# The first attention of a four-layer kernel: division moved behind the weighted values, the first block's scores a turn ahead, and the copies and the rotation dealt anew

## The chip, the cores and the metric

One core of one Trainium2 chip. The metric is the device time of one execution in microseconds (us); before the change it is 1525.61 us, the median of 3 runs (1525.4 to 1527.39). The engines go by their names in the profile: PE is TensorE (PEld its loading of weights), DVE is VectorE, ACT is ScalarE, POOL is GpSimd, SP is the engine that issues most transfers. Each engine works through its own queue in order, and queues meet only in semaphores.

## What is computed

The reference is a network of four layers over 4 sequences of 256 tokens, 512 wide. Each layer is a norm, an attention and a feed-forward part, and they differ. Only the attention of the first layer is touched:

```python
def _L0_attn_ref(x, wq, wk, wv, wo):
    # B, T, C = 4, 256, 512; n_head = 32, h = 16
    q, k, v = (proj(wq), proj(wk), proj(wv))
    q = _apply_rope(q, sin, cos)      # x * cos + rot(x) * sin
    k = _apply_rope(k, sin, cos)
    scores = jnp.einsum('bnth,bnsh->bnts', q, k) * (1.0 / math.sqrt(h))
    scores = jnp.where(causal, scores, -jnp.inf)
    attn = jax.nn.softmax(scores, axis=-1)
    out = jnp.einsum('bnts,bnsh->bnth', attn, v)
    ...
    return jnp.einsum('btc,dc->btd', out, wo)
```

## The kernel before

The program is written by hand, engine by engine, with semaphores; nothing is scheduled by a planner. A phase ends where all engines meet in `finish`. Phase 1 is the first norm, phase 2 the first attention, phase 3 the first feed-forward part.

Phase 2 goes over `NB` = 4 blocks (a block is one sequence of 256 tokens) and, in each, over `G0` = 8 groups `g` of four heads. One group of one block is a turn, `t = 8 b + g`; there are 32. PSUM has 8 banks. A turn uses them so:

- banks 0 and 1: scores of the first 128 tokens (`tb` = 0, the early half, which sees 128 keys); banks 2 and 3: those of the other 128 tokens (`tb` = 1, the late half, 256 keys)
- bank 5, left half: the projection of a unit; right half: the values, or a quarter of the product with `wo` for an earlier block (a "piece")
- banks 5, 6 and 7: the transposed probabilities; banks 6 and 7 also the transposed stacks
- bank 4: the weighted values of a pair of turns, even and odd, four heads each. The first turn of a pair clears the bank and so waits until the last pair was taken away (`ot`).

A unit is the projection of 128 tokens to q or k for half of the heads; `prepared(b, g)` says which unit is made in turn `(b, g)`, five turns ahead of its use. The last five turns of the last block make none. Values are made in turns `g` = 1, 2, 5 and 6 (`VALUES`), pieces in the turns that `quarter` names (3, 4 and 7 of the second block; 0, 3, 4 and 7 of the third; 0 and 3 to 6 of the last).

In a turn of before, PE makes the scores and then masks them with four products (L1544), transposes the probabilities of the turn before (L1526), projects a unit and makes values or a piece (L1573 to L1581), transposes the stacks of the earlier unit (L1477) and makes the weighted values (L1490). ACT copies the first block of transposed probabilities out (`A_pT`, L677), takes the exponentials with their sums (L694), copies the transposed stacks to `qT` or `kT` (L671), the values (L662), the projection with its halves swapped (`A_sw`, L646) and the stack of the rotated unit (L654). POOL multiplies `A_sw` by the sines (L477). DVE takes the row minima (`least`, L1052; the scores are negated, so the minimum is subtracted), the rests of the stack (L1018), the other two blocks of transposed probabilities (L1024), divides the probabilities by their sums (L1061 to L1066), adds a piece to `X` (L1030), multiplies by the cosines (L1005, `A_T1`, which the profile calls `A_T`) and adds sines and cosines (L1011, `A_q`), and every second turn copies the weighted values to `OT0` (L1042).

Copies on ACT all go through one helper and so all have the line L598. The products of the projection have the lines L347 to L349 of `product3`. The second `OT0` and the second buffer of probabilities lie in `raw` and go by that name in the profile.

SP stages the normed tokens of the next block once the last unit that reads the old ones is projected (L369), and starts to load the weights of phase 3 when all units are projected (L404). In the last block DVE, POOL and ACT also prepare the first weights of phase 3 (`unpack`, `scale_tile`, `ffn_heads`, `weight_rests`).

Of the kernel before, what the change touches and what calls it, by code (L numbers as in the profile page):

```python
# [13 lines left out]
def build_program(nc, d, out):  # L14
# [8 lines left out]
    P = 128  # L23
    C = 512
# [24 lines left out]
    with ctx:  # L49
# [41 lines left out]
        with phase() as early:  # L91
# [3 lines left out]
            zq = sb(early, "zq", [NF, C], I32)  # L95
# [6 lines left out]
            with phase() as st:  # L102
# [20 lines left out]
                A_sum = sb(st, "A_sum", [P, 8])  # L123
                A_rec = sb(st, "A_rec", [P, 8])
# [153 lines left out]
        a = sems("a", "stage0 stage1 init proj sw t1 t2 q hi lo tp ev vps vcp sc least exp rec pn pt pe pd pv ot wo_ps x")  # L278
# [77 lines left out]
        def _(sp):  # L356
# [12 lines left out]
            def stage(b):  # L369
                for tl in range(2):  # L370
                    if not isinstance(b, int) or b >= 1:
                        sp.wait_ge(a["proj"], b * G0 + (tl - 1))
                    else:
                        ln_wait(sp, 0, "lo", tl + 1)
# [29 lines left out]
            sp.wait_ge(a["proj"], G0 * NB)  # L404
# [53 lines left out]
        def _(pool):  # L458
# [17 lines left out]

            def sines(U, tl, is_k):  # L477
                pool.wait_ge(a["sw"], U + 1)
                nc.gpsimd.tensor_tensor(A_sw[:, :, :], A_sw[:, :, :], rope0s[:, is_k, tl, :].unsqueeze(1).broadcast_to([P, H0 // 2, D0]), ALU.mult)\  # L479
                  .then_inc(a["t2"], 1)  # L480

            def attend(b):
                for g in range(G0):
                    unit = prepared(b, g)
                    if unit:
                        sines(unit[0], *unit[3:])

            for g in FIRST:
                unit = prepared(-1, g)
                sines(unit[0], *unit[3:])  # L490
            for b in range(NB):
                attend(b)

# [102 lines left out]
        def _(act):  # L596
# [49 lines left out]
            def swap_halves(unit):  # L646
                U = unit[0]
                act.wait_ge(a["proj"], U + 1)
                after(act, a["q"], U)
                ps = PS[:, 5, 0:HALF].rearrange("p (h d) -> p h d", h=H0 // 2)  # L650
                copy(A_sw[:, :, 0:D0 // 2], ps[:, :, D0 // 2:D0])
                copy(A_sw[:, :, D0 // 2:D0], ps[:, :, 0:D0 // 2], a["sw"])

            def stack_heads(unit):  # L654
                U, _, _, _, is_k = unit
                act.wait_ge(a["q"], U + 1)
                after(act, a["tp"], U)
                copy(STK[:, :, 0:D0].bitcast(F32R), A_q[:, :, :])
                at = 2 * D0 if is_k else D0
                copy(STK[:, :, at:at + D0].bitcast(F32R), A_q[:, :, :], a["hi"])  # L660

# [1363 lines left out]
```

## Time and profile before

| | |
|---|---|
| median of 3 runs | 1525.61 us (1525.4 to 1527.39) |
| the profiled execution | 1527.51 us |
| its span | 1525.5 us |
| mean granted clock of PE | 0.972 |
| PE busy | 1391.6 us (91%) |
| DVE busy | 1046.1 us (69%) |
| ACT busy | 735.5 us (48%) |
| POOL busy | 433.2 us (28%) |

The profiled execution is one run of its own; rows come from it, so sums are made against its 1527.51 us. "Busy" counts an engine's instructions, overlapping ones once. In a timeline a group of equal instructions stands in one row, with the time of its start and the time from the first one's start to the last one's end; behind it stands the idle time of the engine ahead of the row and the instruction that ended it. Products on PE overlap: one shows about 0.28 us, but the next may start 0.11 or 0.12 us after it. The chain of waits follows the work that ended last back from its end, at each step to what released it. The granted clock is 1.00 at full speed.

### The profile page before, as it was taken

Reading aid. Unit: us, or ns where it says so; the run is one execution under the profiler, and the core shown is the slowest. Engines: PE = TensorE matmul, PEld = TensorE weight load, DVE = VectorE, ACT = ScalarE, POOL = GpSimd, SP = SyncE. Lnnn points to the kernel's source line nnn. Section 1 sums busy time; section 2 is a strip of 40 time slices with the busy share of each in tenths; the row PEclk is TensorE's granted clock in tenths of the full one; section 3 lists DMA queues with packets and bytes.
Section 4 is the critical chain, followed back from the end, with each engine's and each line's share of the span. In section 5 each row is a group of like instructions: output and inputs, shape, how many; then the busy total and the mean of one; then the engine's idle time right before and its main releaser. Section 6 shows DMA issues by size and latency. Waiting matters only on the chain.

```text
span 1525.5 us, 26083 instructions
## 1 busy us (share of the span) xinstructions
PE 1391.6 (91%) x9252; PEld 1202.8 (79%) x9252; DVE 1046.1 (69%) x2049; ACT 735.5 (48%) x1996; POOL 433.2 (28%) x328
## 2 busy tenths in 40 slices
PE   3889999899999696989999999999999999948998
PEld 2777777667777584879898999899998999837887
DVE  6688778959999644456676666676666766763554
ACT  3777777622222222336556565556555665522332
POOL 5100000122222641324343442414343443224000
PEclk9999999989999897799999999999999999979999
DMA  6101020212230001111212120010212120010000
GB/s 207 29 2 29 1 71 2 84 63 102 105 117 0 21 0 35 45 35 28 70 29 69 28 69 27 21 48 28 69 28 69 28 69 28 0 63 7 15 14 28
DMA packets 39687, 67.92 MB, mean 45 GB/s; under 512 B 4940, under 2 KB 13799, under 8 KB 39618
## 3 DMA queue, kind: packets, MB, share of 16 engines
q1 hardware_dynamic: 37522, 65.69, 13.7%
q10 hardware_dynamic: 2096, 1.33, 0.3%
q8 instruction: 41, 0.67, 0.2%
q14 instruction: 28, 0.23, 0.0%
HBM read 60.68 MB, written 2.13 MB: 41 GB/s over the span
## 4 chain that ended last, share of the span: by engine, by line
PE 71%; issue 9%; DVE 8%; ACT 6%; POOL 4%; DMA 1%; SPq 0%; POOLq 0%; DVEq 0%; ACTq 0%
PE PS L347 18%; PE PS L349 17%; PE PS L348 17%; PE PS L1833 2%; PE PS L1482 2%; PE PS L1820 2%; PE PS L1819 2%; PE PS L1818 2%; POOL E_sw L546 1%; DVE ln_xn L937 1%; ACT A_p L694 1%; POOL A_sw L479 1%; PE PS L1522 1%; ACT A_pT L598 1%; PE PS L1426 1%
## 5 line engine op out<-in xcount | busy, mean ns | idle before, releaser
L347 PE MATMUL PS<-XNH,E_WL 128*128 128x256 f32 x768 | 215.8, 281 | 6.6 <-POOL E_WL L462 5.8
L349 PE MATMUL PS<-XNH,E_WH 128*128 128x256 f32 x768 | 214.8, 280 | 0.0
L348 PE MATMUL PS<-XNL,E_WH 128*128 128x256 f32 x768 | 214.3, 279 | 0.0
L546 POOL TENSOR_TENSOR E_sw<-E_sw,rope2s 128x1024 f32<-128x1024 f32 x64 | 105.0, 1641 | 267.6 <-ACT E_sw L598 267.6
L1259 DVE TENSOR_REDUCE E_nb<-PS 128x4 f32<-128x512 f32 x64 | 61.3, 958 | 163.4 <-PE PS L1820 163.4
L347 PEld LDWEIGHTS PS<-XNH,E_WL 128*128 128x128 f32 x768 | 144.5, 188 | 11.0 <-POOL E_WL L462 8.8
L348 PEld LDWEIGHTS PS<-XNL,E_WH 128*128 128x128 f32 x768 | 144.5, 188 | 1.0
L349 PEld LDWEIGHTS PS<-XNH,E_WH 128*128 128x128 f32 x768 | 144.2, 188 | 0.0
L462 POOL TENSOR_TENSOR E_WL<-raw,E_WH 128x512 fp32r<-128x512 f32 x80 | 102.7, 1313 | 131.9 <-ACT E_WH L598 131.9
L598 ACT ACTIVATE E_sw<-PS 64x256 f32<-64x256 f32 (+1 forms) x128 | 89.4, 699 | 104.6 <-PE PS L349 103.1
L808 ACT ACTIVATE E_p<-PS,E_nb 128x128 f32<-128x128 f32 (+1 forms) x256 | 104.2, 420 | 35.4 <-DVE E_nb L1259 35.4
L347 PE MATMUL PS<-E_WH,OL 128*128 128x512 f32 x256 | 103.4, 404 | 1.4 <-DVE OL L1329 1.4
L349 PE MATMUL PS<-E_WH,OH 128*128 128x512 f32 x256 | 100.6, 393 | 0.0
L348 PE MATMUL PS<-E_WL,OH 128*128 128x512 f32 x256 | 100.0, 390 | 0.0
L500 POOL TENSOR_TENSOR F_w<-F_t,scb 128x512 f32<-128x512 f32 x33 | 48.5, 1469 | 133.2 <-DVE F_t L990 133.2
L479 POOL TENSOR_TENSOR A_sw<-A_sw,rope0s 128x256 f32<-128x256 f32 x32 | 23.2, 725 | 212.5 <-ACT A_sw L598 212.5
L1269 DVE TENSOR_SCALAR E_p<-E_p,E_rec 128x128 f32<-128x128 f32 (+1 forms) x256 | 79.7, 375 | 2.3
L598 ACT ACTIVATE PH<-PS 128x512 fp32r<-128x512 f32 x64 | 52.0, 812 | 58.8 <-PE PS L1833 58.8
L1426 PE MATMUL PS<-ident,ln_xn 128*128 128x128 f32 x128 | 29.2, 373 | 52.9 <-DVE ln_xn L937 52.9
L1818 PE MATMUL PS<-QKH,QKL 128*128 128x256 f32 x256 | 74.9, 293 | 0.0
L1820 PE MATMUL PS<-QKH 128*128 128x256 f32 x256 | 72.6, 284 | 0.0
L1312 DVE TENSOR_TENSOR PL<-PS,PH 128x512 fp32r<-128x512 f32 x64 | 61.1, 956 | 16.6 <-ACT PH L598 15.3
(269 smaller groups left out, 4113.3 us busy)
## 6 DMA issues: line engine op xcount, KB each, us to landing
raw<-in_w SPq DMA_DIRECT2D x104, 256.0 KB, 2.9
words<-in_words SPq DMA_DIRECT2D x11, 768.0 KB, 4.2
wo<-in_wo SPq DMA_DIRECT2D x32, 256.0 KB, 3.9
zb<-z_scratch SPq DMA_DIRECT2D x11, 384.0 KB, 4.8
scb<-in_scales SPq DMA_DIRECT2D x11, 384.0 KB, 5.6
X<-in_x SPq DMA_DIRECT2D x8, 256.0 KB, 5.6
SGH<-XNH SPq DMA_DIRECT2D x8, 256.0 KB, 2.7
SGL<-XNL SPq DMA_DIRECT2D x8, 256.0 KB, 2.8
```

Source lines behind the costliest of these rows:

```text
L347: nc.tensor.matmul(o, sl, mh, start=first, stop=False, **shared)
L348: nc.tensor.matmul(o, sh, ml, start=False, stop=False, **shared)
L349: return nc.tensor.matmul(o, sh, mh, start=False, stop=last, **shared)
L462: nc.gpsimd.tensor_tensor(lo, raw[:, slot, :], f32(hi), ALU.subtract).then_inc(w_lo, 1)
L546: nc.gpsimd.tensor_tensor(E_sw[:, heads, :], E_sw[:, heads, :], rope2s[:, :].unsqueeze(1).broadcast_to([P, heads.stop - heads.start, SEQ]) ...
L598: ins = nc.scalar.activation(o, i, ACT.Copy)
L808: last = nc.scalar.activation(E_p[:, blocks, :].rearrange("p n t -> p (n t)"), PS[:, 3 + 2 * tb + h // 2, at:at + (tb + 1) * P], ACT.Exp, ...
L1259: V.tensor_reduce(E_nb[:, 4 * tb:4 * tb + 4], PS[:, 3 + 2 * tb:5 + 2 * tb, :].rearrange("p n (h s) -> p (n h) s", h=2)[:, :, 0:(tb + 1) * ...
L1269: last = V.tensor_scalar(E_p[:, blocks, :], E_p[:, blocks, :], E_rec[:, 4 * tb + h:4 * tb + h + 1], None, ALU.mult)
L1312: V.tensor_tensor(PL[:, n, :], PS[:, 3 + n.start:3 + n.stop, :], f32(PH[:, n, :]), ALU.subtract)\
L1818: mm(o, QKL[:, h, t], QKH[:, 4, :], start=False, stop=False, skip_group_check=True)
L1820: last = mm(o, QKH[:, h, t], QKH[:, 4, :], start=False, stop=True, skip_group_check=True)
```

## The change

- **Division.** The probabilities are no longer divided by their sums. `A_sum` and the new `A_inv` hold the sums of both turns of a pair. After the pair's second turn DVE inverts them (`invert_sums`) and spreads each over 16 columns (`A_rec`, which lies in the enlarged `zq`); PE transposes that into the right half of bank 4 (`sums`, in the even turns); DVE copies the reciprocals into `OT0` and multiplies them by the weighted values (`take_outputs`, now in the odd turns from the fourth on, ahead of `invert_sums`).
- **Scores.** PE makes the masks first and the scores on top. The early half of turn t + 1 is made in turn t, behind the stack transposes; the late half stands at the turn's start. ACT and DVE take their halves in that order.
- **Pieces and values** are made behind the stacks' transposes and the early scores, once the projection has been read. They have signals of their own (`vps`, `wo_ps`).
- **Rotation.** DVE multiplies by sines and cosines straight from PSUM (`turn_heads`); POOL adds (`rotate`) and makes the rests (`stack_rests`); DVE makes both copies of the stack in one instruction (`stack_heads`).
- **Copies.** The values of a turn are copied by DVE, those of the first five units still by ACT.
- SP waits for `vps` in place of `proj`.

The core of the diff:

```diff
 POOL
+            def rotate(unit):
+                U = unit[0]
+                pool.wait_ge(a["t1"], U + 1)
+                pool.wait_ge(a["t2"], U + 1)
+                after(pool, a["lo"], U)
+                nc.gpsimd.tensor_tensor(A_q[:, :, :], A_T1[:, :, :], A_sw[:, :, :], ALU.add).then_inc(a["q"], 1)
+
+            def stack_rests(unit):
+                U, _, _, _, is_k = unit
+                pool.wait_ge(a["hi"], U + 1)
+                at = D0 if is_k else 2 * D0
+                nc.gpsimd.tensor_tensor(STK[:, :, at:at + D0], A_q[:, :, :], STK[:, :, 0:D0], ALU.subtract).then_inc(a["lo"], 1)
 ACT
+            def exponentials(t, tb):
+                e = t % 2
+                act.wait_ge(a["least"], t * 2 + (tb + 1))
+                after(act, a["pt"], t * 2 - 2)
+                if e == 0 and tb == 0:
+                    after(act, a["inv"], t // 2)
...
             def attend(b):
                 for g in range(G0):
+                    t, earlier = b * G0 + g, prepared(b, g, 1)
+                    exponentials(t, 0)
+                    if t:
+                        take_first(t)
+                    exponentials(t, 1)
                     if earlier:
                         take_stacks(earlier)
-                    if unit and g in VALUES:
-                        act.wait_ge(a["proj"], unit[0] + 1)
-                        take_values(unit, 5, 1)
-                    if unit:
-                        swap_halves(unit)
-                        stack_heads(unit)
 DVE
+            def turn_heads(unit):
                 U, _, _, tl, is_k = unit
+                dve.wait_ge(a["proj"], U + 1)
+                after(dve, a["q"], U)
+                ps = PS[:, 5, 0:HALF].rearrange("p (h d) -> p h d", h=H0 // 2)
+                half = D0 // 2
+                for at in (0, half):
+                    ins = V.tensor_tensor(A_sw[:, :, at:at + half], ps[:, :, half - at:D0 - at],
+                                          rope0s[:, is_k, tl, at:at + half].unsqueeze(1).broadcast_to([P, H0 // 2, half]), ALU.mult)
+                ins.then_inc(a["t2"], 1)
+                V.tensor_tensor(A_T1[:, :, :], ps, rope0c[:, is_k, tl, :].unsqueeze(1).broadcast_to([P, H0 // 2, D0]), ALU.mult).then_inc(a["t1"], 1)
...
+                both = STK[:, :, 0:at + D0].rearrange("p h (n d) -> p h n d", d=D0)[:, :, 0:at // D0 + 1:at // D0, :]
+                V.tensor_copy(both.bitcast(F32R), A_q[:, :, :].unsqueeze(2).broadcast_to([P, H0 // 2, 2, D0])).then_inc(a["hi"], 1)
...
+            def take_values(unit, n):
+                _, b, half, _, tl = unit
+                dve.wait_ge(a["vps"], n)
...
             def take_outputs(t):
-                dve.wait_ge(a["pv"], t)
+
                 n = t // 2 - 1
-                V.tensor_copy(OT0s[n // KT % 2][:, n % KT, :], PS[:, 4, 0:SEQ]).then_inc(a["ot"], 1)
+                out = OT0s[n // KT % 2][:, n % KT, :]
+                dve.wait_ge(a["rt"], n + 1)
+                V.tensor_copy(out, PS[:, 4, SEQ:2 * SEQ]).then_inc(a["r"], 1)
+                dve.wait_ge(a["r"], n + 1)
+                V.tensor_tensor(out, out, PS[:, 4, 0:SEQ], ALU.mult).then_inc(a["ot"], 1)
...
+            def invert_sums(t):
+                n = t // 2 + 1
+                dve.wait_ge(a["exp"], t * 2 + 2)
+                V.reciprocal(A_inv[:, :, :, :], A_sum[:, :, :, :]).then_inc(a["inv"], 1)
+                dve.wait_ge(a["inv"], n)
+                after(dve, a["rt"], n - 1)
+                V.tensor_copy(A_rec[:, :, :, :, :], A_inv[:, :, :, :].unsqueeze(4).broadcast_to([P, 2, 4, 2, D0])).then_inc(a["rec"], 1)
 
             def attend(b):
                 for g in range(G0):
...
+                    least(t, 1)
+                    if t:
+                        take_second(t)
+                    if unit:
+                        turn_heads(unit)
+                    if t + 1 < NB * G0:
+                        least(t + 1, 0)
+                    if unit:
+                        stack_heads(unit)
+                    if unit and g in VALUES:
+                        take_values(unit, values_before(b, g) + 1)
+                    elif piece:
+                        add_quarter(*piece, quarters_before(b, g) + 1)
+                    if g % 2 == 1 and t > 1:
+                        take_outputs(t - 1)
+                    if g % 2 == 1:
+                        invert_sums(t)
 PE
+            def sums(t):
+
+                pe.wait_ge(a["rec"], t // 2)
+                for tb in range(2):
+                    last = nc.tensor.transpose(PS[:, 4, SEQ + tb * P:SEQ + (tb + 1) * P],
+                                               A_rec[:, tb, :, :, :].rearrange("p c e d -> p (c e d)"), ident[:, :])
+                last.then_inc(a["rt"], 1)
...
+                    scores(t, 1)
                     if t:
                         probabilities(t, g - 1, earlier, prepared(b, g, 2))
                         pe.wait_ge(a["pe"], t)
                     if unit:
-                        last = project(unit)
-                        if g in VALUES:
-                            last = values(unit)
-                        elif piece:
-                            last = output_quarter(*piece, False)
-                        last.then_inc(a["proj"], 1)
-                    elif piece:
-                        output_quarter(*piece, True).then_inc(a["wo_ps"], 1)
+                        project(unit).then_inc(a["proj"], 1)
                     if earlier:
                         after(pe, a["pd"], t)
                         transposes(earlier)
+                    if t + 1 < NB * G0:
+                        scores(t + 1, 0)
+                    if unit and (g in VALUES or piece):
+                        pe.wait_ge(a["t1"], unit[0] + 1)
+                        pe.wait_ge(a["t2"], unit[0] + 1)
+                    if unit and g in VALUES:
+                        values(unit).then_inc(a["vps"], 1)
+                    elif piece:
+                        output_quarter(*piece, not unit).then_inc(a["wo_ps"], 1)
                     if t:
                         weighted_values(t, (g - 1) % G0, b * KT + (g - 1) // 2)
+                        if g % 2 == 0:
+                            sums(t)
```

## Rows read from the trace of the kernel before

**Rows 1.** Busy time by stretch, the 32 turns: length, PE, PEld, DVE, ACT, POOL, clock, DMA, GB/s.

```profile
52.00:303.00 251.00, 222.54 (x2044) 181.73 (x2042) 206.16 (x522) 182.15 (x707) 23.40 (x30) 0.99 0.10 33
```

**Rows 2.** Chain of waits in one turn: start us, length us, what.

```profile
161.67 0.35 ACT A_sw L598 x2
162.09 0.73 POOL A_sw L479
162.90 0.44 DVE A_q L1016
...
164.00 0.57 ACT A_pT L598
```

**Rows 3.** Timeline of PE, one turn with values: start us, us, what [idle before].

```profile
164.61 0.39 PE L347 MATMUL PS<-WQH,SGL 128*128 128x256 f32 x1 [0.50 <-ACT A_pT L598]
...
167.59 1.03 PE L1482 MATMUL PS<-ident,STK 128*128 128x128 f32 x8
168.56 0.64 PE L1502 MATMUL PS<-A_pT,V 128*32 128x256 f32 x8
...
169.35 0.73 PE L1550 MATMUL PS<-kT,qT 64*128 64x128 f32 x8
170.00 0.61 PE L1555 MATMUL PS<-mask_ts,identb 128*128 128x256 bf16 x4
170.97 1.50 PE L1540 MATMUL PS<-ident,A_p 128*128 128x128 f32 x12 [0.36 <-DVE A_T L1008]
172.98 0.39 PE L347 MATMUL PS<-WQH,SGL 128*128 128x256 f32 x1 [0.50 <-ACT A_pT L598]
```

**Rows 4.** Timeline of PE in a turn of the last block without a unit.

```profile
278.58 1.47 PE L1540 MATMUL PS<-ident,raw 128*128 128x128 f32 x12
279.89 1.97 PE L1522 MATMUL PS<-wo,OT 128*128 128x256 f32 x8
```

**Rows 5.** Timeline of DVE: row minima, `A_pT`, division of four blocks, outputs.

```profile
163.24 1.82 DVE L1052 TENSOR_REDUCE A_nb<-PS 128x4 f32<-128x512 f32 x2
...
165.30 1.22 DVE L1028 COPY A_pT<-PS 128x1024 f32<-128x1024 f32 x1
...
166.64 0.88 DVE L1065 TENSOR_SCALAR A_p<-A_p,A_rec 128x128 f32<-128x128 f32 x4
...
171.60 0.42 DVE L1045 COPY raw<-PS 128x256 f32<-128x256 f32 x1
```

**Rows 6.** Chain of waits: a turn's exponentials, a piece, a copy of stacks.

```profile
84.66 3.17 ACT A_p L694 x16
...
141.33 1.73 PE PS L1522 x8
...
143.97 1.03 ACT kT L598
```

**Rows 7.** Timeline of PE: the scores that begin turns 1, 9 and 29.

```profile
51.55 0.72 PE L1550 MATMUL PS<-kT,qT 64*128 64x128 f32 x8 [1.11 <-ACT kT L598]
...
113.02 0.72 PE L1550 MATMUL PS<-kT,qT 64*128 64x128 f32 x8 [0.37 <-issue]
...
277.48 0.72 PE L1550 MATMUL PS<-kT,qT 64*128 64x128 f32 x8 [0.33 <-ACT kT L598]
```

**Rows 8.** Busy time by stretch, the end of the stage, columns as in rows 1.

```profile
305.00:310.00 5.00, 3.01 (x22) 2.08 (x24) 2.51 (x5) 0.60 (x1) 0.00 (x0) 0.54 0.00 0
310.00:315.00 5.00, 4.37 (x17) 1.88 (x10) 0.42 (x1) 0.00 (x0) 0.00 (x0) 0.50 0.00 0
```

**Rows 9.** Chain of waits: the last product with `wo`.

```profile
311.26 9.28 PE PS L1513 x16
```

**Rows 10.** Timeline of DVE and POOL at the start of phase 3, side by side.

```profile
322.08 0.69 DVE L990 TENSOR_TENSOR F_t<-F_q,zb 128x512 f32<-128x512 int32 x1
322.95 1.44 POOL L500 TENSOR_TENSOR F_w<-F_t,scb 128x512 f32<-128x512 f32 x1 [1.39 <-DVE F_t L990]
323.40 1.53 DVE L990 TENSOR_TENSOR F_t<-F_q,zb 128x512 f32<-128x512 int32 x1
```

More of the change, by code:

```diff
@@ L475, in _ @@
             pool.wait_ge(const_in, 16 * 9)
[L477 to L482, printed above, removed]
+            def rotate(unit):
[9 more added lines that the diff above has]
+                nc.gpsimd.tensor_tensor(STK[:, :, at:at + D0], A_q[:, :, :], STK[:, :, 0:D0], ALU.subtract).then_inc(a["lo"], 1)
+            for g in FIRST:
+                unit = prepared(-1, g)
+                rotate(unit)
+                stack_rests(unit)
+            for b in range(NB):
                 for g in range(G0):
@@ L485, in attend @@
                     if unit:
[L486 to L492, printed above, removed]
+                        rotate(unit)
+                        stack_rests(unit)
             def scale_tile(n, p):
@@ L644, in ffn_heads, with take_values @@
                     copy(FWH[p][:, c, :], F_w[:, c, :], f["hi"])
[L646 to L660, printed above, removed]
-            def take_values(unit, bank, side):
-                U, b, half, _, tl = unit
-                if b >= 1:
-                    act.wait_ge(a["pv"], b * G0 + (4 * half - 4))
-                ps = PS[:, bank, side * HALF:(side + 1) * HALF].rearrange("p (k e j d) -> p k e j d", k=2, e=2, j=4)
+            def take_values(unit):
+                _, _, half, _, tl = unit
+                ps = PS[:, 3, 0:HALF].rearrange("p (k e j d) -> p k e j d", k=2, e=2, j=4)
                 for e in range(2):
@@ L681, in take_probabilities @@
                 copy(A_pT[:, 0:4, :], PS[:, 5, :].rearrange("p (h t) -> p h t", h=4), a["pe"])
+            def exponentials(t, tb):
[4 more added lines that the diff above has]
+                    after(act, a["inv"], t // 2)
+                for h in range(4):
+                    n, at = order(h), (h // 2) * SEQ
+                    blocks = slice(n, n + 1) if tb == 0 else slice(4 + 2 * n, 6 + 2 * n)
+                    ins = nc.scalar.activation(A_ps[e][:, blocks, :].rearrange("p n t -> p (n t)"),
+                                               PS[:, 2 * tb + h % 2, at:at + (tb + 1) * P], ACT.Exp, scale=-1.0,
+                                               bias=A_nb[:, 4 * tb + n:4 * tb + n + 1], accum_out=A_sum[:, tb, h, e:e + 1])
+                ins.then_inc(a["exp"], 1)
@@ L1067, in attend @@
-                    if quarter(b, g):
-                        add_quarter(*quarter(b, g), unit)
-                    if unit:
-                        cosines(unit)
-                        rotate(unit)
-                    if g % 2 == 0 and t:
-                        take_outputs(t)
+                    t, unit, piece = b * G0 + g, prepared(b, g), quarter(b, g)
+                    least(t, 1)
+                    if t:
+                        take_second(t)
+                    if unit:
+                        turn_heads(unit)
@@ L1597, in _ @@
                     transposes(unit)
+            scores(0, 0)
             for b in range(NB):
@@ L1603, in _ @@
             weighted_values(NB * G0, G0 - 1, None)
+            sums(NB * G0)
             pe.wait_ge(a["exp"], 2 * NB * G0)
```

155 lines of the change are left out of this document (60 added, 95 removed).

## The prediction

> **What bounds the kernel now.** I read the windows first. The change touches only the first attention, whose 32 turns lie between 52 and 303 us; there TensorE (PE) is busy 222.5 of 251 us, VectorE (DVE) 206, ScalarE (ACT) 182, GpSimd (POOL) 23, and the granted clock is 0.99 [rows 1]. No engine is full, so the turns are bound by a loop of waits. The chain of waits shows it [rows 2]: after the transposes of the stacks ACT copies the two swapped halves (`A_sw`, 161.67), POOL multiplies by the sines (162.09, 0.73 us), DVE adds (`A_q`, 162.90), ACT copies the stacks and only then, because it works in order, the first block of transposed probabilities (`A_pT`, 164.00), and PE may start the next projection at 164.61. One lap of PE is 172.98 - 164.61 = 8.37 us [rows 3]. PE's rows tell what it does in a lap: 24 products of projection and values 2.98 us, stack transposes 0.97 (167.59 to 168.56), weighted values 0.79, scores 0.65, four masks about 0.43 (0.61 shown, with a tail of some 0.2), 12 transposes of probabilities, and two idle gaps, 0.36 us (it waits for `A_T`, DVE's product with the cosines) and 0.50 us (it waits for `A_pT`) [rows 3]. Where nothing is in the way, the 12 transposes take 279.89 - 278.58 = 1.31 us and the next product follows at once: `A_pT` is ready under them [rows 4]. So a lap without gaps would be 2.87 + 0.97 + 0.79 + 0.65 + 0.43 + 1.31 = 7.0 us, and with the pauses that PE shows between masks and transposes about 7.3 us (estimate, 0.2 to 0.4 of pauses a lap). The change can win at most some 1 us of 8.37 a lap, 33 us in all.
>
> **Part 1, the rotation dealt anew.** ACT loses the swap, the stack copies and the value copies; DVE now multiplies by sines and cosines straight from PSUM (two products of 128 elements, about 0.2 us each by the 0.88 us for four in [rows 5], and one of 0.42), POOL adds and makes the rests (0.73 us each [rows 2]), DVE copies the stacks. Since the transposes of this unit come a turn later, this chain (0.8 + 0.8 + 0.5 + 0.8 = 2.9 us, from 3.6 us after the lap's start) ends near 7.3 us and has until 3.6 us of the next lap: hidden. ACT keeps 3.17 us of exponentials, 0.5 for `A_pT` and 1.0 for the stacks [rows 6]: 4.7 us in a lap, hidden. DVE loses the normalisation (eight instructions, 2.0 us) and holds 1.14 + 1.14 + 0.75 + 0.6 + 0.5 + 0.4, plus 0.65 a turn for outputs and sums: 5.2 us, hidden as a sum. Both gaps of the old lap go: `A_pT` waits now for the transposes and the early exponentials alone, and the cosines lie a turn earlier.
>
> **Part 2, PE's order.** Scores of the late half, transposes of probabilities, projection, stack transposes, early scores of the next turn, values or output piece, weighted values. The same instructions, with two more transposes on even turns (2 x 0.12 = 0.25 us). Even turn with values: 7.3 + 0.25 = 7.56 us. Stack transposes need DVE's copy of the probabilities (1.22 us [rows 5]), which starts 0.1 us after the 12 transposes; the projection that covers it is 1.43 us, so it ends in the same tenth; I charge 0.1 us.
>
> **Part 3, a new wait that takes the place of the old ones.** On odd turns the weighted values open bank 4 anew and wait for `ot`, that is for `take_outputs`. Before, DVE did that late in the even turn, long before. Now it does it in the odd turn itself, behind `take_values` or `add_quarter`, which wait for the values or the piece, and these are PE's instructions directly ahead of the weighted values. So PE finishes the values and stands still while DVE reads them (2 x 0.2), copies the transposed reciprocals (0.42), waits for its own write, multiplies (0.42) and hands over: 0.13 + 0.05 + 0.40 + 0.42 + 0.34 + 0.14 = 1.48 us, and 0.11 for the slower first product after a stop. Sizes are those of `L1045` and `L1065` [rows 5]; the stall can hardly be under 1.2 us, and 2.0 if nothing of DVE's instructions overlaps. It comes on the 15 odd turns from the fourth on: 22 to 24 us of the 33 go again. In the queue behind the waiting PE are the next turn's late scores and transposes; ACT's early exponentials of the even turn also wait, for the reciprocals that stand behind `take_outputs` on DVE, but they end (about 0.6 us into the next lap) before `A_pT` can be taken (1.4 us): no second stall. Odd turn with values: 7.31 + 1.48 + 0.11 = 8.90 us. A pair is 16.46 us against 16.74 before.
>
> **The other turns.** An output piece takes 1.73 us [rows 6] in place of 1.43, so pairs with pieces are 7.86 + 9.13 = 16.99 us. A turn with neither is 6.13 us (even) or 8.12 (odd: there PE is through early and the stall is 2.1 us, since `take_outputs` stands behind the stack copies, ready about 7.2 us into the lap).
>
> **The sum, by stretches.** The scores of the first, ninth and twenty-ninth turn start at 51.55, 113.02 and 277.48 us [rows 7], the last projection into X at 311.26 [rows 9].
> - Up to the first turn: the rotation's POOL part stands behind POOL's four weight rests as before; +0.1 us.
> - First block, 61.5 us. Now 4.4 (first turn, no probabilities) + 7.95 + 7.56 + 8.12 + 6.13 + 8.90 + 7.56 + 8.12 = 58.7: -2.8.
> - Turns 9 to 28, 164.5 us. The four turns that begin the second block take 6.13 + 8.90 + 7.56 + 9.13 = 31.7, and four more groups 7.86 + 8.90 + 7.56 + 9.13 = 33.45 each, the last 0.2 longer: 165.7: +1.2. The gain of part 1 and the new wait cancel here.
> - Last four turns and the way out, 33.8 us. These have no projection; DVE with unpacking and weight rests sets them today. Without the normalisation they take 5.5 + 6.8 + 5.5, and the last turn to the output 10.2, since the last transposes no longer wait for DVE's division, while the outputs take one more copy and product (0.5 us): 28.0 us, -5.8. In this 1.8 us is that I reckon at the full clock, where today the granted clock falls to 0.54 and to 0.50, the lower of its two levels, after PE had stood idle for a third of the time [rows 8].
> Together -7.2 us. If the clock falls as today, -5.4; if it stays up through the 16 products of 9.28 us [rows 9], of which the later ones run 0.43 us apart and the first five 0.85, two us more, -9.3. I take -7.1. The profiled execution took 1527.51 us (span 1525.5): it becomes 1520.4, and as it stands 1.9 us above the median of the runs, 1525.61, my time is 1518.5.
>
> **Sharing between DVE and POOL.** A DVE product of two SBUF operands took 0.69 us alone and 1.53 us beside a POOL product, which itself was 1.44 us [rows 10]. POOL now works twice a turn instead of once. The DVE work beside it is the early row minima, the value copies and the outputs, all read from PSUM; only the copy of the reciprocals reads SBUF, and it starts 1 us after POOL's rests. I charge nothing; in the first units the zero points' three instructions meet POOL's additions, at most 1.5 us, under PE's projections.
> The Trainium skill (GPSIMD Engine Reference, section 8, Key points) says that GpSimd shares its SBUF interfaces with VectorE, with contention for instructions in a 2-port mode or with two SBUF inputs. The trace agrees, with the 0.69 and 1.53 us above; by the rule the chain of part 3, fed from PSUM, stays as reckoned, and the sum is the same. It speaks against the change only if the stack copies (SBUF to SBUF) meet POOL, which their waits exclude.
>
> **The rivals.** (a) PE's own waits cost more than I charge. The pause between masks and transposes differs by up to 0.2 us with the number of waits; PE now has two or three more in a turn. 32 x 0.2 = 6.4 us more gives 1524.9, no difference. For it: the pauses exist [rows 3]; against it: where 12 or more products precede, waits long met leave no gap (167.59 follows at once).
> (b) The slower side: the stall of the odd turns is 2.3 us or more, because DVE's four steps meet POOL's rests after all, at the price of 1.53 - 0.69 = 0.84 us each: 15 x 0.84 = 12.6 us, 1531.1. From a stall of 2.15 us the kernel is slower by over 3 us (7.1 + 3.0 = 10.1 = 15 x 0.67). For it: POOL's rests run just then (6.5 to 7.2 us into the lap); against it: PSUM operands, and the second row of DVE's chain starts after 7.1.
> (c) The stall is 1.2 us, the pauses are as in the fastest places (0.1 a turn), the clock stays up: -4.2 - 3.2 - 2.2 more, 1509.
> (d) The change does what it says and no more: without the new wait 24 us would be won, 1495. The order of the two queues speaks against it; 1 in 50, in (c) below.
>
> **How the numbers follow.** Forecast 0.50, (a) 0.22, (b) 0.15, (c) with (d) 0.13. Time 1518.5 us. The range takes in (c) and (b): 1507 to 1532. What this kernel's measurement can tell from no change is about 0.2%, 3 us. Faster by more: the forecast nearly whole (0.46), (c), and a few of (a): 0.61. Within: 0.23. Slower: 0.16.
>
> **What would show it.** In the profile after: PE idle 1.2 to 1.6 us before the weighted values (the 128x256 products with 32 rows of `A_pT`) on odd turns and on no even one, put down to DVE's writing of `OT`; no idle before the projection; laps of 7.6 and 8.9 us in turn; early exponentials on even turns released by the reciprocals. Wrong would be: idle before the stack transposes of more than 0.2 us, idle before the 12 transposes, odd stalls over 2 us, or a DVE row of the chain over 0.5 us; or middle turns clearly under 8.2 us on the mean.

## The result and the profile after

The changed kernel takes 1529.93 us (median of 8 runs, 1528.88 to 1531.98), the kernel before beside it on the same chip 1526.14 us (8 runs): a ratio of 1.0022, 95% interval 1.0013 to 1.0031. It is slower by 3.8 us, just over the 0.2% that the prediction called measurable. Forecast were 1518.5 us and "faster"; the time lies in the range of 1507 to 1532, near its upper end. The profiled execution took 1529.9 us with a span of 1527.7.

Turns now begin with the masks of the late half, so stretches are counted from there (before: from the first scores, [rows 7]):

| stretch | before | predicted | after |
|---|---|---|---|
| first block, eight turns | 61.5 | 58.7 | 61.8 |
| turns 9 to 28 | 164.5 | 165.7 | 172.7 |
| last four turns and the way out | 33.8 | 28.0 | 29.0 |
| last product to the start of phase 3 | 10.1 | 10.1 | 7.9 |

The windows of the profile after, as in [rows 1] and [rows 8]:

```profile
52.00:303.00 251.00, 227.25 (x2033) 186.75 (x2032) 159.63 (x304) 154.00 (x558) 43.16 (x57) 0.99 0.09 27
305.00:310.00 5.00, 2.80 (x34) 2.14 (x35) 4.26 (x7) 2.55 (x10) 0.00 (x0) 1.00 0.36 141
310.00:315.00 5.00, 2.53 (x31) 1.79 (x29) 2.07 (x3) 0.60 (x1) 0.00 (x0) 1.00 0.00 0
```

DVE fell from 206 to 160 us and ACT from 182 to 154, POOL rose from 23 to 43, as dealt. PE is busy 5 us more in the same stretch and idle for 24 in place of 28, and that idleness stands in other places. What PE waited for in 52 to 315 us (line <- releaser: us in total, times, longest), and, below, what ACT waited for in 52 to 303 us:

```profile
PE PS L1509 <- DVE OT L1044: 12.6, 8, 2.0
PE PS L1509 <- DVE raw L1044: 10.7, 7, 2.2
...
ACT A_p L681 <- DVE A_inv L1055: 38.3, 15, 3.0
```

L1509 is the first of the weighted values, L1044 the multiplication in `take_outputs`: 15 stops, 23.3 us. The old gaps ([rows 3], 0.36 and 0.50 us a lap) are gone. The early exponentials do wait for the reciprocals, but nobody waits for them.

Two turns of PE: an even one with a piece from 182.10 and an odd one with values from 190.30.

```profile
182.10 0.39 PE L1571 MATMUL PS<-mask_ts,identb 128*128 128x256 bf16 x2
...
190.30 0.38 PE L1571 MATMUL PS<-mask_ts,identb 128*128 128x256 bf16 x2
190.61 0.50 PE L1575 MATMUL PS<-kT,qT 64*128 64x256 f32 x4
191.04 1.53 PE L1556 MATMUL PS<-ident,A_p 128*128 128x128 f32 x12
192.38 0.38 PE L348 MATMUL PS<-WQH,SGL 128*128 128x256 f32 x1
192.61 0.28 PE L349 MATMUL PS<-WQL,SGH 128*128 128x256 f32 x1
192.72 0.28 PE L350 MATMUL PS<-WQH,SGH 128*128 128x256 f32 x1
...
193.91 1.07 PE L1489 MATMUL PS<-ident,STK 128*128 128x128 f32 x8
194.82 0.38 PE L1571 MATMUL PS<-mask_ts,identb 128*128 128x256 bf16 x2
195.13 0.44 PE L1575 MATMUL PS<-kT,qT 64*128 64x128 f32 x4
...
198.65 0.64 PE L1509 MATMUL PS<-A_pT,V 128*32 128x256 f32 x8 [1.46 <-DVE raw L1044]
199.08 0.43 PE L1512 MATMUL PS<-A_pT,V 128*32 128x128 f32 x8
199.44 0.39 PE L1571 MATMUL PS<-mask_ts,identb 128*128 128x256 bf16 x2
```

From start to start the odd turn is 9.14 us (predicted 8.90), the even one with a piece 8.20 (7.86). DVE in the same 1.6 us, with the chain that PE stands behind: values copied (L1025), transposed reciprocals copied (L1042), multiplied (L1044), and only then the next pair's reciprocals.

```profile
197.23 0.49 DVE L1025 COPY V<-PS 128x128 f32<-128x128 f32 x2 [0.59 <-PE PS L350]
197.63 0.41 DVE L1042 COPY raw<-PS 128x256 f32<-128x256 f32 x1
198.08 0.42 DVE L1044 TENSOR_TENSOR raw<-raw,PS 128x256 f32<-128x256 f32 x1
198.42 0.25 DVE L1055 RECIPROCAL A_inv<-A_sum 128x16 f32<-128x16 f32 x1
```

The last product begins at 315.00 and takes 7.12 us, against 9.28 before [rows 9], since the granted clock is 1.00 (the windows above) where it had been 0.54 and 0.50 [rows 8]. In an odd turn with neither values nor a piece the stop is 2.00 us (2.2 in the very last turn), and twice the clock fell behind it:

```profile
79.58 0.74 PE L1509 MATMUL PS<-A_pT,V 128*32 128x256 f32 x8 [2.00 <-DVE OT L1044]
...
81.94 2.22 PE L1556 MATMUL PS<-ident,raw 128*128 128x128 f32 x12
```

```profile
81.00:86.00 5.00, 5.00 (x35) 4.48 (x34) 2.82 (x4) 2.64 (x11) 0.00 (x0) 0.76 0.00 0
...
113.00:119.00 6.00, 6.00 (x48) 5.46 (x41) 2.81 (x4) 3.54 (x16) 0.00 (x0) 0.72 0.00 1
```

Twelve transposes that take 1.53 us at the full clock take 2.22 here and 2.76 at 114.02. The two turns that begin at 80.67 and 113.26 last 7.5 and 7.8 us; 6.13 was predicted.

### The profile page after: what moved, and what is told of

It is laid out like the page before. It is cut to its first block, busy times and chain, and to the rows that moved or that the text cites. A ratio compares the mean times of both kernels' runs of the same rounds, so it can differ in the third digit from the quotient of the medians.

```text
span 1527.7 us, 25850 instructions
## 1 busy us (share of the span) xinstructions
PE 1398.4 (92%) x9284; PEld 1211.1 (79%) x9284; DVE 1003.9 (66%) x1837; ACT 706.9 (46%) x1840; POOL 456.9 (30%) x360
## 4 chain that ended last, share of the span: by engine, by line
PE 78%; DVE 8%; issue 7%; POOL 3%; ACT 2%; DMA 1%; SPq 0%; POOLq 0%; DVEq 0%; ACTq 0%
PE PS L348 18%; PE PS L350 17%; PE PS L349 17%; PE PS L1556 3%; PE PS L1853 2%; PE PS L1489 2%; PE PS L1839 2%; PE PS L1838 2%; PE PS L1840 2%; PE PS L1575 2%; PE PS L1537 2%; POOL E_sw L553 1%; PE PS L1509 1%; DVE ln_xn L922 1%; PE PS L1571 1%
## 5 line engine op out<-in xcount | busy, mean ns | idle before, releaser
L1048 DVE TENSOR_REDUCE A_nb<-PS 128x4 f32<-128x512 f32 x64 | 61.3, 958 | 56.1 <-PE PS L1575 56.0
L1839 PE MATMUL PS<-QKL,QKH 128*128 128x256 f32 x256 | 72.7, 284 | 0.0
```

Of the source, the lines that this page charges most:

```text
L1048: V.tensor_reduce(A_nb[:, 4 * tb:4 * tb + 4], PS[:, 2 * tb:2 * tb + 2, :].rearrange("p n (h s) -> p (n h) s", h=2)[:, :, 0:(tb + 1) * P], ...
L1839: mm(o, QKH[:, h, t], QKL[:, 4, :], start=False, stop=False, skip_group_check=True)
```

## The experiments

All ratios are to the kernel before, with the 95% interval. "Middle" means 113 to 250 us. The kernel before, measured again beside each set of runs, had medians of 1526.1 to 1527.2 us (1529.7 beside the two single profiles at the end), so differences of about 1 us between experiments are left open.

### Take the outputs out of PE's way

The stop of 1.46 us has its cause in where `take_outputs` stands in DVE's queue, not in its work. The weighted values of the pair are complete at the end of the even turn, so it can stand at the head of the odd turn, while PE transposes. The first edit:

```diff
 DVE attend, turn t
+                    if g % 2 == 1 and t > 1:
+                        take_outputs(t - 1)
                     least(t, 1)
...
-                    if g % 2 == 1 and t > 1:
-                        take_outputs(t - 1)
```

> One move in the changed kernel: on odd turns DVE takes the outputs (two instructions, 0.8 us) at the turn's start, in the 1.3 us that it idles there, instead of behind the copy of the values. Theory S (the stall on the odd turns, 1.40 to 1.46 us on PE and 23 us in all, comes from that place in DVE's queue and is the whole of what ate the gain): the idle time of PE ahead of the weighted values goes, the time falls by 20 to 24 us, to about 1507. Rival R1 (the stall only stands for something else that is late next, DVE's row minima, the copy of the values or ACT's early exponentials, which still wait for the reciprocals): PE's idle time moves ahead of the transposes or the projection, and less than 8 us are won, 1522 or more.

1505.37 us, ratio 0.9858 (0.9842 to 0.9875): 24.6 us less than the changed kernel, and 1.4% faster than before. Theory S held. DVE takes the outputs as soon as PE has transposed the sums, and PE does not stop before the odd turn's weighted values:

```profile
193.11 0.43 DVE L1042 COPY OT<-PS 128x256 f32<-128x256 f32 x1 [0.67 <-PE PS L1520]
193.57 0.42 DVE L1044 TENSOR_TENSOR OT<-OT,PS 128x256 f32<-128x256 f32 x1
...
200.04 0.64 PE L1509 MATMUL PS<-A_pT,V 128*32 128x256 f32 x8
```

The turn from 192.91 to 200.83 lasts 7.92 us where it had 9.38. The 24.6 us hold more than the stops: the two falls of the clock behind them (3.0 us, below) are gone as well. Against that, the turns from 79.02 and 107.34 us last 6.81 us, where the changed kernel needs 6.27 for such a turn at the full clock (from 113.40 in its second profile). In the middle PE is now full and its clock at 1.00:

```profile
113.00:250.00 137.00, 137.00 (x1245) 112.75 (x1244) 93.57 (x184) 87.51 (x316) 25.93 (x36) 1.00 0.09 29
```

The second edit also moves `invert_sums`, so that the early exponentials wait less.

```diff
 DVE attend, turn t (with the first edit)
                     if unit:
                         turn_heads(unit)
+                    if g % 2 == 1:
+                        invert_sums(t)
                     if t + 1 < NB * G0:
                         least(t + 1, 0)
...
-                    if g % 2 == 1:
-                        invert_sums(t)
```

> As the kernel with the outputs first, and on odd turns DVE inverts the sums right after the rotation's products, ahead of the early row minima. ACT's early exponentials of the even turns are then no longer released by the reciprocals (idle 2.7 to 3.0 us on ACT). Theory S: those 3 us were hidden, so within 1.5 us of the kernel with the outputs first, about 1507. Rival R1: they are late next once the stall is gone; another 5 us or more are won here.

1504.41 us, 0.985 (0.9833 to 0.9866). No difference that can be told from the first: that wait of ACT, 38 us in all, was hidden, but for 0.38 us in each of the two turns just named (6.43 now in place of 6.81). The copy of the reciprocals now runs beside POOL's addition and takes 0.76 us in place of 0.29; PE waits for it nowhere. This kernel, "both early", is the base of the next ones.

### What the moved division is worth

Both early, with the division back on the probabilities, and neither transposed sums nor the multiplication at the outputs:

```diff
+            def divide(t, tb):
+                e = t % 2
+                dve.wait_ge(a["exp"], t * 2 + (tb + 1))
+                V.reciprocal(A_inv[:, tb, :, e], A_sum[:, tb, :, e]).then_inc(a["rec"], 1)
+                dve.wait_ge(a["rec"], t * 2 + (tb + 1))
+                for h in range(4):
...
+                    ins = V.tensor_scalar(A_ps[e][:, blocks, :], A_ps[e][:, blocks, :], A_inv[:, tb, h, e:e + 1], None, ALU.mult)
+                ins.then_inc(a["pn"], 1)
 DVE attend
+                    divide(t, 0)
                     least(t, 1)
```

> Outputs early, but the division back on the probabilities, ahead of the weighted values, as before the change (late half's behind the copies of the values, early half's at the next turn's start), without the transposed reciprocals. DVE then holds 5.2 - 0.7 + 2.4 = 6.9 us a turn, in order, and PE's transposes wait for it. Theory D (the division's move is what lets the turn come down to PE's 7.7 us): laps of 8.3 us or more, 1520 to 1530. Rival: DVE's sum still fits under PE's lap, and the move is worth little: 1508 or less.

1540.44 us, 1.0086 (1.0064 to 1.0108), 36.0 us more than both early: theory D, though the time lies above its 1520 to 1530. Turns in the middle take 8.4 to 9.0 us. Between the two profiles, the way to the ninth turn is 10.8 us longer, turns 9 to 28 are 17.6 longer, and the last turns up to the last product 8.8. DVE is busy 199 of 251 us and PE waits for its copy of the probabilities before the stacks' transposes, which in the changed kernel never happened in the middle:

```profile
PE PS L1489 <- DVE A_pT L1015: 18.8, 25, 1.1
...
52.00:303.00 251.00, 221.99 (x1956) 177.84 (x1955) 199.44 (x546) 147.49 (x531) 41.63 (x56) 0.99 0.09 27
```

So the division was rightly moved; the new wait hid its worth. The 36 us hold for this place in DVE's queue; no other place for the division was tried.

### The scores a turn ahead

Both early, with the early half back at its own turn's start (on ACT behind the first block of `A_pT`):

```diff
 PE attend
+                    scores(t, 0)
                     scores(t, 1)
...
-                    if t + 1 < NB * G0:
-                        scores(t + 1, 0)
```

> The kernel with outputs and sums early (1504.4 us), and the early half of the scores back at its own turn's start, ahead of the late half; ACT takes A_pT first again. Theory S: in a turn of 7.6 us the exponentials end 1.5 us before the next scores need their banks, so the turn ahead buys nothing there and only the five short turns at the end lose 0.5 to 1 us each: 1507 to 1510. Rival: the exponentials are late next without it, in every turn: 0.5 us or more in each, 1520 or more.

1513.81 us, 0.9924 (0.9906 to 0.9941): 9.4 us more than both early, where 3 to 6 were expected. Phase 3 starts at 307.35 in place of 298.09. Three parts show. Up to the tenth turn 1.1 us are lost. The next 18 turns take 0.18 us more each, 3.2 in all, though PE idles in neither kernel; the stacks' transposes are shorter when masks follow them than when a piece does. Both early, then this kernel (PE, one turn each):

```profile
195.51 1.06 PE L1489 MATMUL PS<-ident,STK 128*128 128x128 f32 x8
196.42 0.38 PE L1571 MATMUL PS<-mask_ts,identb 128*128 128x256 bf16 x2
```

```profile
198.41 1.07 PE L1487 MATMUL PS<-ident,STK 128*128 128x128 f32 x8
199.48 2.00 PE L1535 MATMUL PS<-wo,raw 128*128 128x256 f32 x8
...
291.22 2.79 PE L1554 MATMUL PS<-ident,raw 128*128 128x128 f32 x12 [0.75 <-ACT raw L681]
```

From start to start 0.91 against 1.07 us. The rest, 5.0 us, lies in the last turns and the way out, where no projection covers a chain: two waits more, of 1.34 and 0.75 us, and a clock that falls (last row: 2.79 us for twelve transposes). In the middle, no wait of PE depends on the turn ahead.

### The masks' place

What I had under-reckoned was PE's own work. Masks behind the scores, once in the changed kernel and once on both early:

```diff
 scores(t, tb)
-                for e in range(2):
...
-                    mm(seen, identb[:, :], mask_ts[...], start=True, stop=False)
                 for h in range(4):
...
-                    last = mm(..., start=False, stop=(h >= 2))
+                    mm(..., start=(h < 2), stop=False)
+                for e in range(2):
...
+                    last = mm(seen, identb[:, :], mask_ts[...], start=False, stop=True)
```

> The changed kernel with the two masks of each half behind its scores, as before the change, instead of ahead of them. PE's masks and scores take 0.31 + 0.43 and 0.31 + 0.37 = 1.42 us a turn now, against 1.08 us of work and 0.1 to 0.2 of pauses before. Theory M (the order costs it: a mask ahead of the scores takes 0.155 us instead of 0.107): 0.1 to 0.2 us less a turn, 3 to 6 us in all, about 1526. Theory G (the splitting into two groups costs it: each change of shape costs PE about 0.1 us whatever the order): no change within 1.5 us, 1530.

> Outputs and sums early, and masks behind the scores. Behind the stall of the changed kernel the masks' place was worth 5 us (1524.7 against 1529.9). Theory M (it is work of PE, which sets the turn in either kernel): 5 us again, 1499. Rival: with the stall gone DVE or ACT sets the turn, or the masks' price was only a wait: under 2 us.

1524.74 us, 0.9992 (0.9977 to 1.0008), 5.2 us less than the changed kernel; and 1499.87 us, 0.9819 (0.9793 to 0.9846), 4.5 less than both early and the fastest here. The times are those of theory M both times; its account, a cheaper mask, is only a part of it. From the first of the two:

```profile
185.39 0.50 PE L1572 MATMUL PS<-kT,qT 64*128 64x256 f32 x4
185.82 0.39 PE L1576 MATMUL PS<-mask_ts,identb 128*128 128x256 bf16 x2
186.05 1.47 PE L1556 MATMUL PS<-ident,A_p 128*128 128x128 f32 x12
...
188.88 1.06 PE L1489 MATMUL PS<-ident,STK 128*128 128x128 f32 x8
189.87 0.44 PE L1572 MATMUL PS<-kT,qT 64*128 64x128 f32 x4
190.24 0.39 PE L1576 MATMUL PS<-mask_ts,identb 128*128 128x256 bf16 x2
190.38 0.36 PE L348 MATMUL PS<-WQH,SGL 128*128 128x256 f32 x1
```

The late half's two masks take 0.23 us from start to start here and 0.31 ahead of the scores (190.30 to 190.61 above). The early half's take 0.14 ahead of values (190.24 to 190.38), 0.23 ahead of a piece, and 0.32, no less than ahead of the scores, where the weighted values follow at once. The neighbours change too: the transposes of the probabilities take 1.29 us in place of 1.34 and a piece 1.82 in place of 1.93, but the stacks' transposes 0.99 in place of 0.91 and the transposed sums 0.37 in place of 0.28. The scores themselves take as long as before, 0.43. In sum an odd turn is 0.22 or 0.23 us shorter, an even one 0.13 or 0.14, and an even turn with neither values nor a piece 0.07 longer; over all turns, at the full clock, that is 4.3 us.

### The pieces' place

Values and pieces directly behind the projection, where DVE waits for them before it reads either; once on the changed kernel, once on both early:

```diff
 PE attend
                     if unit:
                         project(unit).then_inc(a["proj"], 1)
+                    if unit and g in VALUES:
+                        values(unit).then_inc(a["vps"], 1)
+                    elif piece:
+                        output_quarter(*piece, not unit).then_inc(a["wo_ps"], 1)
                     if earlier:
                         after(pe, a["pd"], t)
                         transposes(earlier)
 DVE attend
+                    if unit and g in VALUES:
+                        dve.wait_ge(a["vps"], values_before(b, g) + 1)
+                    elif unit and piece:
+                        dve.wait_ge(a["wo_ps"], quarters_before(b, g) + 1)
                     if unit:
                         turn_heads(unit)
```

> The changed kernel with values and pieces back directly behind the projection, ahead of the stacks' transposes; DVE waits for them before it rotates. Theory S: the outputs on DVE then no longer wait for the values; they still stand behind the stack copies, so the stall on odd turns shrinks from 1.45 to about 0.7 us (11 us in all), and PE saves one slow first product (0.1 us) on 22 turns: 12 to 14 us less, about 1517. Rival: the later rotation (1.5 us) is late next, at the stack copies and so at the outputs: the stall stays at 1.3 us or more, and the time within 4 us of 1530.

> Outputs and sums early, and values and pieces directly behind the projection. The run with the pieces back alone was 22 us slower than the changed kernel, with a stall of 2.33 us on odd turns and a granted clock of 0.91 in the stage. Theory C (that loss was the longer stall at outputs that stand behind the rotation, and the clock that fell with it; the late rotation harms nothing else): without the stall the clock stays at 1.00, PE saves 0.1 us on 22 turns, 1502 to 1504. Rival L (the rotation, late by 1.5 us, is itself what holds PE): 1512 or more, with PE idle ahead of the stacks' transposes or the projection.

The first took 1552.38 us, 1.0158 (1.0141 to 1.0175), 22.5 more than the changed kernel where 12 less were expected. I had thought that the outputs would come earlier once the piece did; but they stand behind the rotation, and this now waits for the piece:

```profile
190.69 0.49 DVE L997 TENSOR_TENSOR A_sw<-PS,rope0s 128x128 f32<-128x128 f32 x2 [2.02 <-PE PS L1541]
...
194.44 0.64 PE L1513 MATMUL PS<-A_pT,V 128*32 128x256 f32 x8 [2.33 <-DVE raw L1044]
...
52.00:303.00 251.00, 221.30 (x1886) 185.84 (x1885) 140.30 (x276) 139.10 (x504) 39.38 (x54) 0.91 0.09 26
```

The stops grow to 2.33 and 2.40 us in the turns with values or a piece, 33.9 us in 15 turns against 23.3. That is 10.6 us more. The granted clock stands at 0.91 over the 32 turns in place of 0.99, and turns of the same kind show its price: an even turn with a piece lasts 7.98 us at the full clock (from 195.23) and 10.11 behind a fall (from 154.74). Of the ten stops of 2.33 or 2.40 us seven were followed by a fall; behind three, ahead of the turns from 195.23, 213.08 and 250.22, the clock stayed up. (The profiled run, 1556.87 us, is the slowest of the four; the share of the clock in the median was not measured.)

In the second, without stops, nothing of that loss is left: 1502.75 us, 0.9849 (0.983 to 0.9868), theory C, clock 1.00 in 113 to 250 us. The ratio is that of both early, 0.985, so the 1.7 us between the medians are not shown to be a gain. The turns explain it: odd ones are 0.22 us shorter (7.69 in place of 7.91 with a piece), even ones no shorter with a piece and 0.06 longer with values, since there the transposes of the probabilities start 0.20 to 0.31 us late. They write bank 5, and DVE, behind its late rotation, reads the values or the piece out of it until just before:

```profile
182.34 0.48 DVE L1025 COPY V<-PS 128x128 f32<-128x128 f32 x2
...
182.91 1.50 PE L1560 MATMUL PS<-ident,raw 128*128 128x128 f32 x12 [0.23 <-issue]
```

On these turns the copy of the reciprocals, 0.76 us beside POOL, stands in the same stretch of DVE's queue; which of the two makes the pause was not separated.

The Trainium skill (TensorE: Matmul & The Clock Gate, HAM oscillation) says that idle stretches of TensorE inside a loop can throttle it anew in every round. The two kernels agree with that in part: with the same products in the same order the clock is 0.90 in 113 to 250 us with the stops and 1.00 without, but it fell behind seven of those ten stops, not behind every one.

### All three together

Both early, the pieces back and the masks last:

> The changed kernel with three edits together: the outputs taken at the odd turn's start (and the sums inverted behind the turned heads), the values and pieces directly behind the projection with the rotation waiting for them, and the masks behind the scores. Alone on top of the early outputs (1504.4 us), the second gave -1.7 us and the third -4.5 us. Theory A (each saves first products and pauses of TensorE in its own place, and TensorE stays full through the middle): they add up, 1504.4 - 1.7 - 4.5 = 1498.2 us, 1497 to 1499.7, ratio to before about 0.981; PE idle in 113 to 250 us stays 0 and the laps of turns with a piece come to about 7.7 us. Theory B (the gain of the pieces' place came at the breaks beside the masks, which the masks' new place has already taken, or the rotation's wait now shows because the turn is shorter): 1499.9 us or more, no better than the masks' edit alone, with an idle before the projection or the scores.

1502.28 us, 0.9844 (0.9829 to 0.9858): 2.4 us above both early with the masks last, theory B. (The intervals of the two ratios overlap; the single runs, 1501.8 to 1504.9 and 1494.5 to 1501.3, do not.) The two edits do not add up. PE, then DVE:

```profile
197.74 0.39 PE L1580 MATMUL PS<-mask_ts,identb 128*128 128x256 bf16 x2
198.06 0.64 PE L1513 MATMUL PS<-A_pT,V 128*32 128x256 f32 x8
...
199.30 0.39 PE L1580 MATMUL PS<-mask_ts,identb 128*128 128x256 bf16 x2
199.70 0.55 PE L1560 MATMUL PS<-ident,raw 128*128 128x128 f32 x3
...
199.24 0.41 DVE L1031 TENSOR_TENSOR X<-X,PS 128x256 f32<-128x256 f32 x1
```

DVE reads the piece out of bank 5 until 199.65, behind its late rotation, and the transposes, which write that bank, start at 199.70: 0.40 us behind the masks' start, where it is 0.23 with masks last alone. But this pause is the one that the pieces' place had already brought, above. What is lost is the gain on the early masks: the weighted values now follow them at once, and they take 0.32 us (197.74 to 198.06) where they took 0.15 ahead of values and 0.23 ahead of a piece. So the odd turns are no shorter than with the masks last alone (7.38 and 7.65 us against 7.39 and 7.69), and the even ones are longer by the pause (8.05 and 8.29 against 7.75 and 8.06).

### Does a stop of 2.00 us always bring the clock down?

In the first profile of masks last the clock was 1.00 behind the same two stops. So both kernels were profiled once more, unaltered:

> The changed kernel unaltered, one more profile. In its first profile the granted clock was 0.76 in 81 to 86 us and 0.72 in 113 to 119 us, behind the two stops of 2.00 us, and the two turns that begin there took 7.5 and 7.8 us in place of 6.3. Theory F (the falls belong to these stops but do not come each time): this profile lacks one or both, the turn then takes 6.3 us, and its span is 1.2 to 2.7 us shorter than the first profile's, 1525.0 to 1526.5. Theory G (every stop of 2.00 us brings the clock down in this order of products, and only the masks' place took the falls away): both falls stand again, span 1527.7 +- 0.5 us.

> The changed kernel with the masks behind the scores, unaltered, one more profile. In its first profile the granted clock was 1.00 in 81 to 86 us and in 113 to 119 us, behind the same stops of 2.00 us. Theory F (the falls come and go): a fall may stand here in either place, with 1.2 to 1.5 us more for its turn, span 1522.7 to 1525.5. Theory G (this order of products keeps the clock up): both places at 1.00 again, span 1522.7 +- 0.5.

1530.98 us (span 1528.8) and 1525.77 us (span 1523.6), one run each. The changed kernel's windows, then masks last's:

```profile
81.00:86.00 5.00, 5.00 (x31) 4.78 (x32) 2.54 (x3) 2.84 (x12) 0.00 (x0) 0.66 0.00 0
...
113.00:119.00 6.00, 6.00 (x67) 4.95 (x60) 3.55 (x6) 4.66 (x18) 0.73 (x1) 1.00 0.02 5
```

```profile
81.00:86.00 5.00, 5.00 (x32) 4.85 (x31) 2.46 (x3) 3.03 (x13) 0.00 (x0) 0.66 0.00 0
...
113.00:119.00 6.00, 6.00 (x54) 5.04 (x46) 3.11 (x5) 3.68 (x17) 0.00 (x0) 0.78 0.01 1
```

The falls come and go in either kernel, theory F: behind eight such stops in four profiles the clock fell five times and stayed up three times. The turn from 113.4 us took 6.3 us in the second profile, against 7.8 in the first. The span expected by theory F was missed (1528.8, not under 1526.5): a fall elsewhere took back what this one gave, the clock being 0.91 in 300 to 320 us and the last product 8.63 us, and the phases behind the attention took 1.0 us more. So whole spans of single profiles cannot tell what the masks' place is worth. Turns can: from the tenth to the 28th, at the full clock in all four profiles, the changed kernel takes 164.9 and 164.8 us, masks last 161.4 and 161.3. These 3.5 us are not the clock's.

## Why the prediction went wrong

**Right: the mechanism, its place and its size.** Part 1 (the old gaps go, rotation and copies hidden), and part 3: 15 stops on odd turns, none on even ones, 1.40 to 1.46 us (1.48 reckoned), 2.0 to 2.2 in turns with neither (2.1), 23.3 us in sum (22 to 24). The run with the outputs first gave 24.6 us back, 3.0 of them the clock's. The last turns gained their 5 us (29.0 us against 28.0 predicted), and the last product its 2.2 us, which the -9.3 variant held and I did not take; that part is chance, since in the second profile of the same kernel this product took 8.63 us.

**The step that failed is part 2, what PE itself needs in a turn.** I took the old lap's products, 7.0 us, and added 0.3 for pauses. The 7.0 was itself 0.1 short: projection and values are 2.98 us in my own row (164.61 to 167.59) and 2.87 in my sum. The pauses went, but the products did not stay as they were. In the odd turn above: masks and scores 0.74 + 0.68 = 1.42 us in place of 1.08; projection and values 1.53 each, 3.06 in place of 2.87; the transposes of the probabilities 1.34 in place of 1.31, the stacks' 0.91 in place of 0.97. That is 0.5 us more, of which the charge for pauses covered 0.3; a piece takes 1.93 us in place of 1.73. Laps came out 0.24 us longer on odd and 0.34 on even turns. Four masks in one go behind eight scores had cost 0.43 us [rows 3]; two and two, ahead, cost 0.62. The masks-last runs put 0.13 to 0.23 us a turn, 4.5 to 5.2 us in all, down to the order of masks and scores; the rest, scores 0.80 in place of 0.65 and longer first products where one kind of product follows another, was read from rows and not separated.

**A second, smaller one: the clock in the middle.** I reckoned with a fall only at the end. The falls behind the two stops of 2.00 us cost 1.5 us each in the first profile: turns of 7.5 and 7.8 us in place of 6.3, and, right behind the first stop, 0.3 us on the weighted values (1.09 us from 79.58 to 80.67, against 0.78 in the second profile).

The sum closes: against the forecast the first block has 3.1 us more (1.5 of clock, 1.6 in eight turns), turns 9 to 28 have 7.0 (1.5 of clock, 5.5 in twenty turns), the last four turns 1.0, the last product 2.2 less: 8.9, where the profiled execution is 9.5 above its forecast of 1520.4.

**The rivals.** (a) had nearly the right size (6.4 us of PE's own time; 8.1 were measured: 1.6, 5.5 and 1.0) but it put this into pauses that were not there, and ended 5 us short. (b) did not come: no DVE row of the chain is over 0.5 us. (c) was wrong on the stop and, in the first profile, right on the clock at the end. (d), the change without its new wait, was put at 1495 and measures 1504.4, again high by the products I had under-reckoned; I had given it 1 in 50 as a result of this change, which it was not. The direction hung on -7 us as the difference of two terms of 30 and 24 us, and an error of 0.3 us in a turn of 8 was enough to turn it; 0.61 for "faster" was too much for that.

## What to carry to other kernels

Before placing a step in an engine's in-order queue, ask who waits for its result and what that one issued last: here `take_outputs` stood behind an instruction that waits for PE's latest product, while PE waited for `take_outputs`, and moving one call to an idle slot turned +0.2% into -1.4%. When a change splits or reorders groups of small products, price each group again by rows with the same neighbours, since the 0.1 us at every border, 32 turns long, is as much as the gain looked for. When a bound engine is full, the order of its own instructions is the next thing to try.

## What the runs showed of the hardware

- What a few small products take depends on what follows. Two masks (128x256, bf16) take 0.31 us ahead of four scores (64 rows, f32); behind the scores they take 0.23 us ahead of transposes or a piece, 0.14 ahead of values and 0.32 ahead of the weighted values. Eight transposes of the stacks take 0.91 us when masks follow, 0.99 when scores do and 1.07 when values or a piece do.
- The first product after another kind takes longer: 0.23 us to the next start in place of 0.12 (192.38 to 192.61 above). A piece takes 1.93 us behind masks and scores and 1.73 directly behind a projection.
- A DVE copy of 128x256 from SBUF to SBUF took 0.29 us alone and 0.76 beside an addition of POOL.
- The granted clock stayed at 1.00 through stops of 1.4 us, one in each pair of turns. It fell behind five of eight stops of 2.00 us, and behind seven of ten of 2.33 or 2.40 us. A profile more of the same kernel showed the falls elsewhere: a clock term of 1 to 3 us belongs in the range, not in the sum.
